# Graph, mixer and gated-FFN layer on one core: one strided VectorE sum for four additions, and layer-normed rows written by ScalarE

## What is computed

```
xn = layernorm(x)                                   # x: 6250 x 256
low  = relu(segment_sum(edge_weight    * (xn @ weight_low )[dst]))   # 106250 edges, summed by src
high = relu(segment_sum(edge_weight_n2 * (xn @ weight_high)[dst]))
mlp  = relu(xn @ weight_mlp)
att  = softmax(sigmoid([low@a_low, high@a_high, mlp@a_mlp]) @ att_vec / 3)
gnn  = 3 * (att0 * low + att1 * high + att2 * mlp)
mix  = linear attention of 8 heads over all rows (k and v layer-normed), then gelu(. @ w1 + b1) @ w2 + b2 + xn
x    = x + gnn + mix
x    = x + ffn(layernorm(x))                        # top half of the rows by a score, gelu(. @ w1 + b1) @ w2 + b2, times the score
```

## Time and profile before

| | |
|---|---|
| median of 3 runs | 1971.31 us (1970.63 to 1973.62) |
| profiled execution | 1968.29 us, its span 1966.5 us |
| busy in the span | TensorE 1567.2, VectorE 1239.8, ScalarE 915.6, GpSimd 1376.8 us |
| last scatter issued, first gather issued | 764.21 us, 771.51 us |

### The profile page before, as it was taken

How to read it: one execution, slowest core, us unless ns; L and a number is a source line. 1 busy time by engine, 2 the same in 40 slices (tenths; PEclk the granted TensorE clock), 3 DMA queues, 4 the chain that set the end, 5 groups by cost and what they waited for, 6 DMA issues and landing times.

```text
span 1966.5 us, 30490 instructions
## 1 busy us (share of the span) xinstructions
PE 1567.2 (80%) x9109; PEld 1327.7 (68%) x9109; DVE 1239.8 (63%) x3136; ACT 915.6 (47%) x2641; POOL 1376.8 (70%) x1351
## 2 busy tenths in 40 slices
PE   3788888599998561788889888888888888889871
PEld 3466666588877561577777777777777777777750
DVE  8899999879988730345544554455454545545546
ACT  1688888677877550133333343333333334333323
POOL 4337778777777776777777777777777777777700
PEclk9899999789999785799999999999999999999975
DMA  3222221111121003433333333333333333333303
GB/s 89 83 66 68 68 68 49 40 36 47 48 66 47 6 6 95 133 102 105 100 102 103 104 101 105 105 101 100 102 103 103 102 103 105 100 102 105 103 14 131
DMA packets 102212, 162.99 MB, mean 83 GB/s; under 512 B 32190, under 2 KB 72762, under 8 KB 102040
## 3 DMA queue, kind: packets, MB, share of 16 engines
q0 software_dynamic: 55232, 113.59, 20.6%
q1 hardware_dynamic: 46808, 47.29, 7.6%
HBM read 139.76 MB, written 21.04 MB: 82 GB/s over the span
## 4 chain that ended last, share of the span: by engine, by line
POOL 31%; issue 13%; DMA 9%; DVE 2%; PE 2%; SPq 2%; ACT 1%; DVEq 0%; POOLq 0%; ACTq 0%
POOL arena L665 31%; DMA arena<-xn_rows,arena 9%; PE bank L1525 2%; SPq L558 1%; ACT side L1516 1%; POOL sorted_records L648 1%; DVE arena L1246 0%; DVE arena L1248 0%; DVE arena L1119 0%; DVE arena L1113 0%; SPq L563 0%; SPq L561 0%; DVE base L1288 0%; DVE arena L1253 0%; DVE arena L1245 0%
## 5 line engine op out<-in xcount | busy, mean ns | idle before, releaser
L1525 PE MATMUL bank<-arena 128*128 128x128 f32 (+3 forms) x6320 | 1145.1, 338 | 146.8 <-DVE arena L1119 74.4
L1525 PEld LDWEIGHTS bank<-arena 128*128 128x128 f32 (+1 forms) x6320 | 982.5, 188 | 287.8 <-issue 143.2
L665 POOL DMA_INDIRECT arena<-xn_rows,arena x852 | 840.7, 987 | 267.1 <-issue 246.1
L648 POOL DMA_INDIRECT sorted_records<-arena x448 | 512.9, 1145 | 218.0 <-issue 138.0
L1119 DVE TENSOR_TENSOR arena<-arena 128x640 f32<-128x640 bf16 (+1 forms) x204 | 164.4, 806 | 29.1 <-DVE arena L1113 0.2
L1113 DVE SCALAR_TENSOR_TENSOR arena<-io,arena 128x320 bf16<-128x320 f32 (+1 forms) x204 | 97.6, 479 | 96.5 <-issue 44.4
L1164 DVE CUSTOM_DVE_ANT_0 arena<-arena 128x256 f32<-128x256 f32 x98 | 37.8, 423 | 166.2 <-ACT arena L1449 166.2
L1169 DVE SCALAR_TENSOR_TENSOR att_prod<-sg,att_neg 128x9 f32<-128x9 f32 x49 | 8.4, 171 | 212.0 <-ACT sg L1457 212.0
L1525 PE MATMUL bank<-arena,base 128*128 128x128 f32 (+3 forms) x766 | 118.0, 287 | 22.0 <-ACT base L1304 13.8
L1525 PEld LDWEIGHTS bank<-arena,base 128*128 128x128 f32 (+2 forms) x766 | 110.2, 212 | 23.2 <-ACT base L1304 14.4
L1487 ACT ACTIVATE arena<-bank 128x256 f32<-128x256 f32 x49 | 18.8, 383 | 228.6 <-PE bank L1525 228.6
(11 more groups left out here) (311 smaller groups left out, 1918.2 us busy)
## 6 DMA issues: line engine op xcount, KB each, us to landing
arena<-xn_rows,arena POOLq DMA_INDIRECT x852
sorted_records<-arena POOLq DMA_INDIRECT x448
arena<-in_x SPq DMA_DIRECT2D x12, 512.0 KB, 4.1
xn_rows<-arena SPq DMA_DIRECT2D x12, 512.0 KB
x_plus_xn_rows<-arena SPq DMA_DIRECT2D x12, 512.0 KB
arena<-x_plus_xn_rows SPq DMA_DIRECT2D x12, 512.0 KB, 3.9
arena<-xn_rows SPq DMA_DIRECT2D x12, 512.0 KB
out<-base SPq DMA_DIRECT2D x4, 1024.0 KB
```

The source lines that it names most:

```text
L648: pool.indirect_dma_start(rec_dram, bass.IndirectOffsetOnAxis(ap=idx[0:PR, par, u:u + 1], axis=0), stage_rec[0:PR, par, u * 8:(u + 1) * 8] ...
L665: pool.indirect_dma_start(gring[:, c % GR, :], None, xn_dram, bass.IndirectOffsetOnAxis(ap=rring[:, c, 3:4].bitcast(I32), axis=0)).then_in ...
L1525: return pe.matmul(out_, lhsT, rhs, start=start, stop=stop, **kw)
```

## The change

Three things: the sum over ten columns is one `tensor_reduce` over a view in which the column j is innermost (neighbours along it lie 98 bf16 apart); the layer-normed rows are written by ScalarE, `rs * x + (-mean * rs)`, from the scale and shift that VectorE computes; the semaphores follow.

```diff
-        many = r1.take([P, GROUPS, GS // 2, NB], BF16)
+        many = r1.take([P, GROUPS, NB], BF16)
...
-                h = oh[:, :, :].rearrange("p (s j) b -> p s j b", s=GROUPS)
-                H = GS // 2
                 with nc.allow_low_precision(reason="whole numbers up to ten"):
-                    dve.tensor_tensor(many[:, :, :, :], h[:, :, 0:H], h[:, :, H:GS], ALU.add).then_inc(S("many_set"), 1)
-                    dve.wait_ge(S("many_set"), 4 * g + 1)
-                    dve.tensor_tensor(many[:, :, 0:2], many[:, :, 0:2], many[:, :, 2:4], ALU.add).then_inc(S("many_set"), 1)
-                    dve.wait_ge(S("many_set"), 4 * g + 2)
-                    dve.tensor_tensor(many[:, :, 0], many[:, :, 0], many[:, :, 1], ALU.add).then_inc(S("many_set"), 1)
-                    dve.wait_ge(S("many_set"), 4 * g + 3)
-                    dve.tensor_tensor(many[:, :, 0], many[:, :, 0], many[:, :, 4], ALU.add).then_inc(S("many_set"), 1)
+                    dve.tensor_reduce(many[:, :, :], oh[:, :, :].rearrange("p (s j) b -> p s b j", s=GROUPS), AX.X, ALU.add).then_inc(S("many_set"), 1)
...
                 dve.wait_ge(S("ln_aggr"), FOUR * a + m)
+                wait(dve, S("xn_ready"), a)
                 dve.tensor_scalar(sd4[:, 0, 0:m], mv4[:, 0:m, 1], EPS, None, ALU.add).then_inc(S("ln_var"), 1)
-            def ln_apply(a, par):
+            def ln_factors(a):
...
-                dve.wait_ge(S("ln_rs"), a + 1)
-                if not (isinstance(a, int) and a == 0):
-                    dve.wait_ge(S("xn_stored"), 32 * a)
-                    dve.wait_ge(S("xt_done"), 2 * a)
+                dve.wait_ge(S("ln_rs"), 2 * a + 1)
+                wait(dve, S("xx_ready"), a)
                 dve.tensor_scalar(sx4[:, 0, 0:m], sd4[:, 0, 0:m], 1.0, None, ALU.add)
-                dve.scalar_tensor_tensor(sx4[:, 1, 0:m], mv4[:, 0:m, 0], -1.0, sd4[:, 0, 0:m], ALU.mult, ALU.mult)
-                for t in range(m):
-                    ins = dve.tensor_scalar(xs[:, t, :], xl[:, par, t, :], mv4[:, t, 0:1], sd4[:, 0, t:t + 1], ALU.subtract, ALU.mult)
-                ins.then_inc(S("xn_ready"), 1)
+                dve.scalar_tensor_tensor(sx4[:, 1, 0:m], mv4[:, 0:m, 0], -1.0, sd4[:, 0, 0:m], ALU.mult, ALU.mult).then_inc(S("ln_rs"), 1)
...
+            def ln_rows(a, par):
+
+                act.wait_ge(S("ln_rs"), 2 * a + 2)
+                wait(act, S("xn_stored"), 32 * a)
+                wait(act, S("xt_done"), 2 * a)
+                for k in range(tiles_of(a)):
+                    ins = act.activation(xs[:, k, :], xl[:, par, k, :], ACT.Identity, bias=sx4[:, 1, k:k + 1], scale=sd4[:, 0, k:k + 1])
+                ins.then_inc(S("xn_ready"), 1)
...
                 if more:
                     copy_rank(g + 1)
+                if ln is not None:
+                    ln_rows(ln, 1 - par)
...
-                pe.wait_ge(S("many_set"), 4 * g + 4)
+                pe.wait_ge(S("many_set"), g + 1)
...
-                mm(R, before[:, :], many[:, :, 0, :], False, False, skip_group_check=True)
+                mm(R, before[:, :], many[:, :, :], False, False, skip_group_check=True)
```

More of the change, by code:

```diff
@@ L931, in slot @@
                 if ln is not None:
-                    ln_apply(ln, 1 - par)
+                    ln_factors(ln)
                 if isinstance(g, int) and g == MIX + 1:
@@ L1083, in _ @@
             wkv_weights()
-            ln_apply(0, 0)
+            ln_factors(0)
             destinations(0, 0)
@@ L1417, in _ @@
             stage_records(0, 0)
+            ln_rows(0, 0)
             schedule(act, slot)
@@ L1533, in ranks @@
                 mm(R, ones_f[0:NB, :], diag[0:NB, :].unsqueeze(1).to_broadcast([NB, GROUPS, NB]), True, False, skip_group_check=True)
-                mm(R, before[:, :], many[:, :, 0, :], False, False, skip_group_check=True)
+                mm(R, before[:, :], many[:, :, :], False, False, skip_group_check=True)
                 for s in range(GROUPS - 1):
-                    ins = mm(R[:, (s + 1) * NB:], ones_b[:, :], many[:, s:s + 1, 0, :].to_broadcast([P, GROUPS - 1 - s, NB]),
+                    ins = mm(R[:, (s + 1) * NB:], ones_b[:, :], many[:, s:s + 1, :].to_broadcast([P, GROUPS - 1 - s, NB]),
                              False, s == GROUPS - 2, skip_group_check=True)
```

## The result

The changed kernel takes **2023.41 us** (median of 4 runs, 2021.53 to 2026.82), the kernel before 1972.39 (4 runs): ratio 1.0261, 95% interval 1.0243 to 1.0279, 51 us slower. The profiled execution took 2026.82 us, its span 2025.1 us. Against the profiled execution of before (span 1966.5) that is 58.6 us. The profiled execution of before is faster than its median and that of the changed kernel slower than its own, so the traces show 7 to 8 us more than the medians do.

The account below looks back on a forecast made before the run. VectorE bounds the sort up to batch 14, then GpSimd until VectorE's cushion is used up. 26 x 4.15 - 42.3 = +65.6 us, taken as +65 on the median 1971.3, gives 2036 us; range 2007 to 2056.

Parts of the forecast that it names:

- What bounds: In the sort, VectorE's time sets the end up to batch 14's addresses; from there GpSimd's, with VectorE about 30 us ahead.
- 16 d: Delay of batch 14's addresses from sixteen reduces; d is VectorE's extra time a batch for the sum, forecast 4.15 us.
- at double time: On VectorE, the reduce jumping 196 bytes was taken at about two cycles an element: 6.27 us instead of 3.2.
- 26 d - 42.3: Shift of the last scatter if VectorE binds to batch 24, d being the sum's added time a batch: +65.6 us forecast.
- The start: First slot: transposes wait for quad 0's rows on ScalarE, 1.97 us added to the path and 1.29 us saving not gained.
- The change of bound: Mixer slots of 24.5 us exceed GpSimd's 23.7, so the cushion is used up and the bound passes from GpSimd to VectorE.
- The rows: Layer-norm rows moved from VectorE to ScalarE: -14.5 us on VectorE, +2.0 us at the start, together -12.5 us.
- No cost inside the slots: Layer-norm slots: ScalarE's added 1.97 us a quad fits, its 6.7 us chain against VectorE's 7.7, 1.0 us to spare.
- (a): Rival: the reduce pays no price for the jump, 1.1 us a batch on VectorE, +5 us, 1976 us; chance 0.10.
- (b): Rival: a one-input reduce holds GpSimd's scatters less, up to 0.6 us a batch, -8 us, 1966 us; chance 0.05.
- (c): Rival: the forecast plus ScalarE's chain exceeding its spare time, up to 1 us more in each of eleven slots, 2047 us; chance 0.05.
- The signs named: Expected in the trace: reduce 5.7 to 6.3 us, GpSimd waiting before nearly every batch up to 24, VectorE not waiting for square roots.

Follow-up runs that it names:

- early-only: Kernel before with the one reduce for batches 0 to 16 only, the four additions from batch 17: 2024.23 us, ratio 1.0254.
- sum-only: Kernel before with the one reduce alone, layer norm untouched: 2036.43 us, ratio 1.0309.
- the probe: Kernel before with scratch reduces and a copy added at VectorE's end, at several element distances: for 2940 bf16, 3.22 us for neighbours, 5.07 at 98 apart.
- late-only: Kernel before with the one reduce for batches 17 to 27 only, layer norm as before: 1982.31 us, ratio 1.0056.

## Why the prediction was right, and where it was not

- **What bounds**: right up to batch 14. The early-only run gives 50.6 us and sum-only 46.2 for 16 d = 49.8, and 16 x 3.11 - 12.5 + 443.2 = 480.5 stands against L818 at 481.14. That it comes so near is partly chance, with single traces some 4 us apart.
- **The reduce**: right in mechanism, 1.04 us too long (6.27 forecast, 5.22 measured), so d = 3.11 and not 4.15. The step that failed is "at double time": I explained L707's 1.9 ns an element away as a head start and took two full cycles. The price at 196 bytes is 0.63 to 0.68 ns an element, not 1.04. L707's own 0.86 is near what the probe shows for words of 4 bytes, which L707 reads (0.80 at 392 bytes); bf16 is cheaper, and the trace of before had no row for it. All of the forecast's excess comes from here: 26 x 1.04 = 27 us, while with d = 3.11 the sum is 26 d - 42.3 = +38.6, or 2010 us.
- **What the sum then lacks**, 12 us in the medians: it puts the last scatter at 764.2 + 38.6 = 802.8, and it came at 811.95, 9.1 us later: 0.6 by batch 14, 6.1 from there to batch 24 (GpSimd's 24.44 us a batch) and 2.4 in the last four. The rest is in the gathers. The start was mis-sized twice, in opposite directions: from L1101 at 67.88 to L1089 at 74.90 are 7.0 us. 1.5 of them are batch 0's reduce (sum-only and the changed kernel with quad 0 on VectorE have this copy at 69.42), where the sum has d = 3.11; 5.5 are the rows and TensorE's lower clock, where it has 2.0. These are single traces: in the late-only kernel, which has no reduce there, the copy stands at 69.37, with a granted clock of 0.72 from 58 to 63 us.
- **The change of bound**: wrong. VectorE's mixer slot is 23.42 us and would allow GpSimd its old 23.7; GpSimd waits for addresses up to batch 15 only. It stays the bound behind batch 14, 0.75 us a batch slower, most of it because of where its scatters fall. The forecast took GpSimd's pace as fixed. With d near 3 the two regimes touch, so the sum went little wrong.
- **Luck in the number**: 2036 us lies only 13 us above the measured 2023 because two errors cancel in part, 27 us too much for the reduce and 12 us that the sum lacks.
- **The rows**: -12.5 forecast, -12.0 by the times and -8.1 at the last scatter, both beside the reduce. "No cost inside the slots" holds only there. The 1.0 us to spare on ScalarE was figured for VectorE's chain of L870; the chain that binds without the reduce goes over TensorE's permute of the third group, which I did not follow.
- **Rivals**: (a) fell by the reduce's duration. (b)'s mechanism is there, at 0.22 us a batch, but its gain needs GpSimd's other scatters to stay where they were. (c) did not show with the long reduce (in the layer-norm slots VectorE waited for ScalarE once, 0.3 us) and did without it.
- **The signs named**: layer-norm slots 26.34 (27.4), mixer slots 23.42 (24.5), last scatter 811.95 (829), GpSimd idle 2.0 us a layer-norm slot beside its gap (3 to 4), mostly off by the one mis-sized term. By the prediction's own sign, GpSimd issuing without a wait from batch 14 on, its picture of the late batches was wrong from batch 16 on.

## What to carry to other kernels

Price a strided read by the byte distance along its innermost axis: here a bf16 reduce at 16 bytes or more cost 1.6 to 1.7 times one of neighbours. A reduce of neighbours is itself slower than additions over contiguous rows (1.04 ns for each element read, against 0.93 us for 1470 results), so four additions of 2.04 us in all beat one reduce of 5.22. Where two engines run at nearly the same pace, taking work off one gains nothing; to see it beforehand, look at the other's time from batch to batch and not at its busy share. Moving work onto a third is free only while the longest stays longest. A wait for TensorE's input costs more than its length when the clock falls behind it (at the start, products of 3.62 us instead of 1.88 behind a wait of 2.33).

## What the runs showed of the hardware that was not expected

- The price of distance is flat from 16 bytes on (5.26 us at 16, 5.28 at 32, for 2880) and a little less at 196 bytes in groups of ten (5.07 for 2940) than in groups of thirty (5.38). In the sort the same reduce takes 5.22 us, 0.15 more than by itself; why is open.
- A scatter that VectorE holds ends 0.83 us after the instruction that held it, so the same instruction costs it much or little by the moment at which it begins: 1.22 us under the first L808 before, 2.21 under the same L800 after. GpSimd's batch moves by 3% (23.69 to 24.44 us) with the same work on GpSimd.
- An instruction of one input can hold a scatter as well (the step mask, 1.38 us); neither reduce did (97 scatters begin under L744, all 0.96).
- The same 852 gathers took 840 to 852 us in traces of kernels that are equal there.
- One chip ran the kernel before in 2560 us where the others ran it in 1972.
